# Perceiver kernel: row statistics, key chunks and query blocks placed anew in the two transposed-score cross-attentions

## The reference, cut to what matters

```python
# L0_xattn: 8 heads, context layer-normed, mask, latents among the keys
xn = layernorm(ctx, ln_x_g, ln_x_b); ln = layernorm(latents, ln_l_g, ln_l_b)
q = ln @ Wq
k, v = split(concatenate([xn, ln], axis=1) @ Wkv)
sim = where(full_mask, einsum('bhid,bhjd->bhij', q * scale, k) * scale, -max)
out = layernorm(softmax(sim) @ v -> heads joined @ Wo, ln_o_g, ln_o_b)
...
# L1_xattn: 16 heads, plain context, no mask
sim = einsum('bhnd,bhmd->bhnm', x @ W_q, ctx @ W_k) * d ** -0.5
out = (softmax(sim) @ (ctx @ W_v) -> heads joined) @ W_o + b_o
```

## Time and profile before

| what | us |
|---|---|
| median of 3 runs (lowest, highest) | 3229.59 (3226.05, 3232.38) |
| the profiled execution | 3231.05 |
| its span | 3229.3 |
| L0 attention, about | 0 to 590 |
| L1 attention, about | 850 to 1725 |
| the ten other stages | the rest |

### The profile page before, as it was taken

One profiled execution on the slowest core, in us unless ns is written; L12 is line 12 of the kernel. 1 busy time (PEld: TensorE's weight loads), 2 busy tenths in 40 slices (PEclk: granted clock), 3 DMA queues, 4 the chain that ended last, 5 costly groups with the idle time before them and its releaser, 6 DMA issues. The chain is left out here.

```text
span 3229.3 us, 44186 instructions
## 1 busy us (share of the span) xinstructions
PE 2705.7 (84%) x15983; PEld 2112.0 (65%) x15983; DVE 1829.2 (57%) x3672; ACT 1578.5 (49%) x2758; POOL 1319.2 (41%) x994
## 2 busy tenths in 40 slices
PE   5788888635789999999996779496899999999777
PEld 4678878513578888888886456365466666666546
DVE  6676666463364544454443344613778778777462
ACT  3666666211265655565563224232555555555332
POOL 0665665230056566665561016001454454454130
PEclk7899999757899999999998889798999999999975
DMA  3232231021201101011100123112000000000000
GB/s 98 63 94 63 67 89 42 16 28 40 67 21 31 42 22 42 21 42 31 31 11 5 40 65 102 25 43 59 21 22 11 21 21 11 21 21 1 22 1 14
DMA packets 238573, 120.11 MB, mean 37 GB/s; under 512 B 37784, under 2 KB 233024, under 8 KB 238400
## 3 DMA queue, kind: packets, MB, share of 16 engines
q1 hardware_dynamic: 238400, 117.81, 13.7%
HBM read 101.46 MB, written 15.28 MB: 36 GB/s over the span
## 5 line engine op out<-in xcount | busy, mean ns | idle before, releaser
L703 POOL TENSOR_TENSOR L_xattn_held<-L_xattn_held,L_xattn_shift 128x512 f32<-128x512 f32 (+1 forms) x613 | 761.5, 1284 | 621.6 <-ACT L_xattn_shift L632 621.6
L446 PEld LDWEIGHTS L_xattn_acc<-L_xattn_rows,L_xattn_held 128*128 128x128 f32 (+2 forms) x5120 | 642.0, 200 | 68.4 <-DVE L_xattn_mixed L787 36.3
L446 PE MATMUL L_xattn_acc<-L_xattn_rows,L_xattn_held 128*128 128x129 f32 (+2 forms) x5120 | 654.2, 284 | 26.9 <-DVE L_xattn_mixed L787 17.8
L1387 POOL TENSOR_TENSOR L_xattn_projected<-L_xattn_along,L_xattn_crossed 128x512 f32<-128x512 f32 (+1 forms) x256 | 271.4, 1068 | 383.0 <-DVE L_xattn_crossed L1428 383.0
L613 ACT ACTIVATE L_xattn_held<-L_xattn_held 128x512 f32<-128x512 f32 (+2 forms) x640 | 401.6, 631 | 0.3
L606 ACT COPY L_xattn_held<-L_xattn_ring 128x512 f32<-128x512 f32 (+1 forms) x416 | 242.8, 584 | 275.5 <-DVE L_xattn_running L806 259.5
L806 DVE TENSOR_TENSOR L_xattn_running<-L_xattn_ring,L_xattn_running 128x512 f32<-128x512 f32 (+1 forms) x384 | 264.3, 688 | 116.3 <-PE L_xattn_ring L430 98.7
L428 PE MATMUL L_xattn_ring<-L_xattn_queries_hi,L_xattn_keys_hi 128*128 128x512 f32 (+2 forms) x640 | 285.0, 445 | 38.6 <-DVE L_xattn_keys_lo L734 35.5
L430 PE MATMUL L_xattn_ring<-L_xattn_queries_hi,L_xattn_keys_lo 128*128 128x512 f32 (+2 forms) x640 | 256.9, 401 | 0.0
L429 PE MATMUL L_xattn_ring<-L_xattn_queries_lo,L_xattn_keys_hi 128*128 128x512 f32 (+2 forms) x640 | 256.4, 401 | 0.0
L1292 ACT COPY L_xattn_probT<-L_xattn_bank_a 128x512 f32<-128x512 f32 (+2 forms) x320 | 138.9, 454 | 221.4 <-PE L_xattn_bank_a L1124 221.4
(11 more groups left out here) (491 smaller groups left out, 4447.2 us busy)
## 6 DMA issues: line engine op xcount, KB each, us to landing
L_xattn_raw<-in_ctx SPq DMA_DIRECT2D x16, 768.0 KB
context_normalised<-L_xattn_fresh SPq DMA_DIRECT2D x16, 768.0 KB
L_xattn_rows<-context_normalised SPq DMA_DIRECT2D x16, 768.0 KB
L_xattn_fresh<-in_ctx SPq DMA_DIRECT2D x16, 768.0 KB
L_xattn_rows<-in_ctx SPq DMA_DIRECT2D x16, 768.0 KB
L_xattn_staged<-in_ctx SPq DMA_DIRECT2D x16, 768.0 KB
L_xattn_xhat<-context_normalised SPq DMA_DIRECT2D x16, 768.0 KB
L_ffn_w<-in_L_ffn_W SPq DMA_DIRECT2D x1, 2048.0 KB, 8.9
```

What stands on the lines that cost most here:

```text
L446: mm = nc.tensor.matmul(acc[:, c // 2, c % 2 * WIDE:(c % 2 + 1) * WIDE], held[0:n, u % 2, k, c * P:(c + 1) * P], rows[0:n, b % 2, k, :], s ...
L703: nc.gpsimd.tensor_tensor(tile, tile, shift[0:keys_of_tile[k]], ALU.subtract).then_inc(shifted, 1)
L1387: nc.gpsimd.tensor_tensor(projected[:, t % 2, c0:c0 + n], along[:, c0:c0 + n], crossed[:, c0:c0 + n], ALU.add)\
```

## The change

It moves work and leaves its amount as it is, in four parts.

1. `measure` runs one bn_stats beside each of the tiles 0 to 12, in place of 4, 4, 4 and 1 in tiles 8 to 11. `gather_moments` moves to tile 1 of the next unit, behind double buffered moments, and `context_root` from tile 0 to tile 2.
2. Context jobs stand at tiles 5, 7, 9, 11, in place of 6, 8, 10, 12, in both attentions.
3. Query jobs. L0: tiles 2 and 3 of odd units, in place of 4 and 5. L1: all four stood in the two units of an odd batch (4, 5 and 5, 9); they now stand in the two units of the even batch before it (3, 8 and 5, 9).
4. Output in L1: from the first unit of an odd batch to its second one. `mixedT` is double buffered for it.

```diff
--- before.py
+++ after.py
@@ -160,18 +160,18 @@
         b, g = u // NG, u % NG
         jobs = {}
         if 3 <= u <= UNITS + 2:
-            jobs[1] = ("mixed", (u - 3) % NG, (u - 3) // NG % 2)
-        if NG == 2 and g == 0 and b % 2 == 1 and 3 <= b <= BATCHES + 1:
+            jobs[1] = ("mixed", (u - 3) % NG, (u - 3) // NG)
+        if NG == 2 and b % 2 == 1 and 3 <= b and g == (b < BATCHES + 1):
             jobs[3] = ("output", (b - 3) // 2)
         if NG == 1 and b % 2 == 0 and 4 <= b <= BATCHES + 2:
             jobs[3] = ("output", (b - 4) // 2)
         if b + 1 < BATCHES:
             if g == 0:
-                for c, slot in enumerate((6, 8, 10, 12)):
+                for c, slot in enumerate((5, 7, 9, 11)):
                     jobs[slot] = ("context", c)
-            if b % 2 == 1:
-                for q in range(2):
-                    jobs[(4, 5)[q] if g == 0 else (5, 9)[q]] = ("queries", 2 * g + q)
+        if b // 2 + 1 < BATCHES // 2 and b % 2 == 2 - NG:
+            for q in range(2):
+                jobs[((2, 3), (3, 8), (5, 9))[NG - 1 + g][q]] = ("queries", 2 * g + q)
         return jobs
 
     FIRST_JOBS = len(CTX_CHUNKS) + 2 * NG
@@ -203,12 +203,12 @@
         running = s.sb("running", [P, 2, BANK])
         peak, peak_wide, shift = s.sb("peak", [P, TURNS]), s.sb("peak_wide", [P, TURNS, P]), s.sb("shift", [P, BANK])
         rinv = s.sb("rinv", [P, 2, 2])
-        mixed, mixedT = s.sb("mixed", [P, TURNS, D]), s.sb("mixedT", [P, NH, 2, SEQ])
+        mixed, mixedT = s.sb("mixed", [P, TURNS, D]), s.sb("mixedT", [P, 2, NH, 2, SEQ])
         outT, out_bias = s.sb("outT", [P, TOKENS]), s.sb("out_bias", [P, 1])
         fold_qk, fold_vo = s.sb("fold_qk", [P, NH, D]), s.sb("fold_vo", [P, NH, D])
         if normed:
             raw = s.sb("raw", [P, 2, CT, D])
-            moments, mean_var = s.sb("moments", [P, CT, 6]), s.sb("mean_var", [P, CT, 2])
+            moments, mean_var = s.sb("moments", [P, 2, CT, 6]), s.sb("mean_var", [P, CT, 2])
             cstd, crstd = s.sb("cstd", [P, CT]), s.sb("crstd", [P, CT])
             gains, gain_col, shift_col = s.sb("gains", [P, 4, D]), s.sb("gain_col", [P, 1]), s.sb("shift_col", [P, 1])
             own = s.sb("own", [P, TILES, D])
...
@@ -619,7 +619,7 @@
                     for k in step:
                         if u < UNITS:
                             keep_tile(u, k)
-                        if normed and k == 0 and u + 1 < BATCHES:
+                        if normed and k == 2 and u + 1 < BATCHES:
                             context_root(u + 1)
                         if k >= LATER and 1 <= u <= UNITS:
                             exponent(u - 1, k - LATER)
@@ -747,13 +747,13 @@
                 if 0 in tiles:
                     dve.wait_ge(ctx_loaded[b % 2], 32 * (b // 2 + 1))
                 for k in tiles:
-                    nc.vector.bn_stats(moments[:, k, :], raw[:, b % 2, k, :])
-
-            def gather_moments():
+                    nc.vector.bn_stats(moments[:, b % 2, k, :], raw[:, b % 2, k, :])
+
+            def gather_moments(b):
 
                 dve.drain()
                 for k in range(CT):
-                    ins = nc.vector.bn_aggr(mean_var[:, k, :], moments[:, k, :])
+                    ins = nc.vector.bn_aggr(mean_var[:, k, :], moments[:, b % 2, k, :])
                 ins.then_inc(cvar_ready, 1)
 
             def invert_std(b):
@@ -814,6 +814,8 @@
                     dve.drain()
                     nc.vector.tensor_copy(peak_wide[:], over_last(peak[:], P)).then_inc(peak_ready, 1)
                 if normed and u + 1 < BATCHES:
+                    if k == 1:
+                        gather_moments(u + 1)
                     if k == 4:
                         invert_std(u + 1)
                         if u >= 1:
@@ -821,18 +823,15 @@
                         place_std()
                     if 4 <= k <= 7:
                         make_xhat(u + 1, k - 4)
-                if normed and u + 2 < BATCHES:
-                    if 8 <= k <= 11:
-                        measure(u + 2, range(4 * (k - 8), min(4 * (k - 7), CT)))
-                    if k == 12:
-                        gather_moments()
+                if normed and k < CT and u + 2 < BATCHES:
+                    measure(u + 2, range(k, k + 1))
                 job = JOBS[u].get(k)
                 if job is None:
                     return
                 if job[0] == "mixed":
                     dve.wait_ge(spare_full, lane.count() + 1)
                     of_g, of = job[1], job[2]
-                    emptied(nc.vector.tensor_copy(mixedT[:, HALF * of_g:HALF * (of_g + 1), of, :],
+                    emptied(nc.vector.tensor_copy(mixedT[:, of // 2 % 2, HALF * of_g:HALF * (of_g + 1), of % 2, :],
                                                   spare[:].rearrange("p (h i) -> p h i", i=SEQ)))
                 elif job[0] == "output":
                     lane.next()
...
```

9 lines of the change are left out of this document (4 added, 5 removed).

## The result

The changed kernel takes 3287.7 us (median of 4 runs, 3279.13 to 3292.49) against 3227.82 for the kernel before in the same measurement: a ratio of 1.0182, 95% interval 1.0156 to 1.0208. It is slower by some 60 us; 3291 had been forecast, in a range of 3258 to 3335. The profiled execution took 3292.49 us, with a span of 3290.7 and a mean granted clock of 0.899 (before 0.907).

What follows compares the result with a forecast made beforehand. A ScalarE-VectorE loop was taken to bound L0 from tile 5 on and L1 units with context jobs, TensorE the rest. 3231.05 + 64 (L0) - 3 (L1) = 3292, so 3291 us for the median; range 3258 to 3335.

Steps and rivals of the forecast that it cites:

- Plain unit, +2.7: L0 units without query jobs: root, first chunk and other chunks make each 2.7 us longer.
- chunks: L0 plain unit: normalising and a bn_stats behind the first split cost 1.3 us, bn_stats behind later splits 0.4.
- root: L0 plain unit: root behind tile 2 delays the shift copy, +1.0 us after TensorE's lateness absorbs 1.1; bounds 0 and 3.0.
- The statistics: L0: one bn_stats a tile adds 0.2 us at the first step, 0.2 behind the first split, 0.4 behind later ones.
- Query unit, +5.6: L0 units with queries: first query rounding stands behind the root, VectorE's look at tile 3 behind its split; 5.6 us longer.
- Clock, +4: L0 unit starts: all take the longer low-clock form of the sums, 0.5 x 8 = 4 us.
- L1, -3: L1: spreading output and queries gives -0.4 us per four units, seven groups, first and last partly; bounds -6 and +3.
- The last split sooner: L0 last step: without aggregation the last split goes first, TensorE's 41.2 us of waits shrink; all gone gives 3190; 6%.
- The root finds a hole: L0: TensorE leads until tile 5, so the 1.9 us are absorbed in plain units, half in query units; 3266 us; 12%.
- The clock within the units: L0: idle stretches before the third and fourth split bring 1.2 GHz, some 3 us more a unit; 3333 us; 10%.
- The blocked copy: L0 query unit: GpSimd's subtractions block the placing copy for at least 5 us; 3326 us or more; 3%.
- Switches dearer in the open: L0 root: each table switch drags a drain of about a microsecond, root costs 5.3 us, not 3.0; 3323 us; 4%.

Runs made afterwards that it cites:

- the run with the root back: The changed kernel with L0's root ahead of the maxima and aggregation at the last tile, as before the change: 3293.01 us.
- the run with the slots back: The changed kernel with L0's chunks at 6, 8, 10, 12 and queries at 4 and 5, as before the change: 3269.34 us.
- The run with L1 alone: The kernel before with only the L1 part of the change, L0 left as it was: 3235.43 us.
- the kernel with single queries: The kernel before with L1 as changed, but its four query jobs at slots 3 and 3, 5, 9, none sharing a context job's step: 3221.52 us.
- the fastest kernel: "combo" with L0's keeping of the sums moved to tile 12, ahead of the aggregation and the last split: 3167.66 us.
- combo: The kernel before with TensorE's unit-start wait relaxed by the last job, rows scaled before GpSimd's subtractions, and L1 queries one a step: 3202.58 us.

## Why the prediction was right, and where its steps were off

**Plain unit, +2.7.** Measured in the body, +2.4. Its parts: chunks 1.7 forecast, 1.8 measured (5.97 us from tile 5 to 7 against 4.75, and 0.19 in each later step); root 1.0 forecast, 0.6 measured. The statistics were in both, at 0.2 here and there, and by themselves cost nothing.

**Query unit, +5.6.** Measured +5.4 in the body. The mechanism shows as told: VectorE idle 2.98 us ahead of the first query split, tile 7 at 5.97 after tile 5. But it isn't the root's alone: with the root back the body lost only 0.3 net, with 1.0 added for the aggregation, so the queries at 2 and 3 cost some 2.3 us by themselves (33.1 less 1.0, 1.8 and 27.9), and the late root with the old slots costs 2.9 (30.9 less 27.9). Together they cost 3.6, less than their sum. The working had one chain through both and so got the sum right; a split by parts, as in my expectation of the run with the root back, was wrong by 34 us.

**Clock, +4.** This step failed, with the wrong sign. I gave every start the longer form of the sums. Instead the pair's starts got shorter, from 13.7 to 12.9 us: over all fifteen starts 4 us less in place of 4 more, and this is most of why L0 grew by 53 and not by 64; the bodies together gave 56 where 60 had been forecast. The sums of a plain unit's start take what they took (4.54 against 4.59), those of a query unit's 3.8 in place of 5.1 to 5.2, since more of the 1.2 GHz stretch falls ahead of them. The same 24 products took 2.95, 3.81, 4.57, 5.11 or 5.47 us in these kernels, by how much of them the 1.2 GHz stretch covered: nothing in the first, nearly all in the last. The splits ahead had shifted by a few us each time. The Trainium skill, TensorE: Matmul & The Clock Gate, section HAM oscillation — how this bites in real kernels, tells of a wait ahead of every block that puts the start of each on the low clock. The traces of before and after agree: the sums of every start from unit 2 on have such a stretch. Those of the plain starts from unit 4 on in the run with the slots back have none, and what the sum needed was how much of the block pays.

**L1, -3.** Measured +6, outside its bounds of -6 and +3. The four units came out as forecast where the clock held: 30.34, 23.35, 26.53 and 24.60, against 30.3, 23.3, 26.6 and 24.6. By these four, six groups give 2.9 us back, as forecast. Two things were missing: the 1.24 us of low clock behind the shared step in four of the six groups (5.0 us), and the first four units, where "the first and last partly" hid 3.7 us. The three add up to the 5.8 measured. The run with L1 alone had 1.5 us in its first units and three long ones, so the size of both terms differs from kernel to kernel.

**The rivals.** *The last split sooner* fell: TensorE waits 39.9 us in 13 starts. Its price was wrong as well: taking the wait away gave 12 us, not 41, since two others stood right behind. *The root finds a hole* fell with the bodies: the root kept 0.6 of its 1.0 us in plain units. *The clock within the units* showed in L1's shared step, not in L0. *The blocked copy* fell: the placing copy took 0.17 us at 320.56, with GpSimd subtracting from 318. That agrees with the Trainium skill, VectorE: DVE Perf Modes, section Why PSUM operands drop a tier, that such a copy isn't in the two-port mode. *Switches dearer in the open* fell: 3.61 us against 3.62. The Trainium skill, ScalarE: Activation LUTs, section What ACT_TABLE_LOAD costs, gives another 1380 ns of drain for each; neither place shows it.

The right total has luck in it: L0 was 11 us under its forecast, 8 of them in the starts, and L1 9 us over it, errors of opposite sign.

## What to carry to other kernels

Before pricing a wait, list everything that its waiter needs and when each comes: here the last split, the kept sums and the scaled rows came within a microsecond or two of each other, one alone was worth 12 us, and all of them with L1's 9 us were worth 63. Put short work of an in-order engine ahead of the instruction that waits, not behind it, and give each job of a shared bank a step of its own. And don't undo one part of a reordering to learn its price without reading where the other parts then stand.

## What the runs showed of the hardware that I had not expected

TensorE's clock is part of a schedule's result: equal idle times of 2.06 us were followed once by 1.2 GHz and once by 2.4 (1157.67 and 1369.88), which made one unit 1.24 us longer than the same unit elsewhere. A short idle time is no safeguard: in the kernel with single queries the sums at 1005.02 come behind one of 0.48 us and run into the low clock (4.59 us for all 24), those at 1109.89 come behind one of 0.49 and keep 2.4 GHz (2.95 us). What decides between the two, no run here shows.

In the fastest kernel GpSimd's scaling, moved ahead, mostly runs while VectorE is due to copy the maxima, SBUF to SBUF. The copy at a query unit's start in the fastest kernel, and GpSimd's scaling:

```profile
322.91 1.95 DVE L816 COPY L_xattn_peak_wide<-L_xattn_peak 128x512 f32<-128x512 f32 x1
```
```profile
321.11 3.47 POOL L696 TENSOR_TENSOR L_xattn_rows<-L_xattn_rows,L_xattn_gains 128x1664 f32<-128x1664 f32 x1 [3.29 <-DMA L_xattn_rows<-context_normalised]
```

It takes 1.95 us in place of 0.43 and ends 0.29 us after the scaling. Of the sixteen copies in L0, thirteen begin while a scaling runs, take 0.48 to 2.85 us and end 0.28 or 0.29 us after it; the other three, which meet at most its last 0.1 us, take 0.43. In "combo", where most copies come after the scaling has ended, all but two take 0.43. The Trainium skill, SBUF — State Buffer, section Who interferes with whom, has this lock. The copies together are some 10 us longer than 0.43 each; how much of that is on the path, no run shows.
